# A graph network kernel: attention messages made by ScalarE as eight scaled copies per unit, and a one-hot build that reads its numbers from PSUM

## The reference, cut to what matters

```python
xl = x @ W
alpha = leaky_relu(a_src[src2] + a_dst[dst2] + a_edge)
ex = exp(alpha - segment_max(alpha, dst2)[dst2])
p = ex / segment_sum(ex, dst2)[dst2]
out = segment_sum(xl[src2] * p[..., None], dst2) + bias
```

## Time and profile before

| | us |
|---|---|
| median of 3 runs | 9410.33 |
| profiled execution | 9404.12 |
| its span | 9402.4 |
| POOL busy | 6718.0 (71%) |
| PE busy | 5202.7 (55%) |
| DVE busy | 3779.7 (40%) |
| ACT busy | 1844.8 (20%) |

### The profile page before, as it was taken

How to read it: one execution, slowest core, us unless ns; L and a number is a source line. 1 busy time by engine, 2 the same in 40 slices (tenths; PEclk the granted TensorE clock), 3 DMA queues, 4 the chain that set the end, 5 groups by cost and what they waited for, 6 DMA issues and landing times. The chain is left out here.

```text
span 9402.4 us, 110210 instructions
## 1 busy us (share of the span) xinstructions
PE 5202.7 (55%) x29965; PEld 3957.9 (42%) x29966; DVE 3779.7 (40%) x5860; ACT 1844.8 (20%) x2616; POOL 6718.0 (71%) x6802
## 2 busy tenths in 40 slices
PE   2777778777787778877512433424452243252443
PEld 1555555555565556655412322323331132242332
DVE  7444444444444444444412423324351243242436
ACT  1333333333333333333200000000010000000000
POOL 4777777777577777777377777777717777777772
PEclk6888887887777887777655666656665666666666
DMA  5222222222222222222322222222212222222221
GB/s 156 74 78 75 78 76 75 78 75 75 85 76 78 76 78 76 78 76 78 81 62 44 57 49 49 57 44 57 39 28 65 44 56 49 46 59 44 54 42 34
DMA packets 376814, 611.95 MB, mean 65 GB/s; under 512 B 173574, under 2 KB 211194, under 8 KB 374971
## 3 DMA queue, kind: packets, MB, share of 16 engines
q0 software_dynamic: 214032, 332.71, 16.9%
q1 hardware_dynamic: 144556, 255.75, 8.3%
q10 hardware_dynamic: 17945, 19.86, 0.7%
HBM read 575.04 MB, written 32.78 MB: 65 GB/s over the span
## 5 line engine op out<-in xcount | busy, mean ns | idle before, releaser
L1248 POOL DMA_INDIRECT big<-xl_table,idx_stage x3328 | 3335.8, 1002 | 1007.8 <-issue 997.7
L761 POOL DMA_INDIRECT big<-q_table,idx_stage x3328 | 3247.3, 976 | 1025.2 <-issue 953.7
L641 PE MATMUL bank<-zero_bf 1*128 1x512 bf16 (+1 forms) x1456 | 475.3, 399 | 2391.5 <-DVE wide L1369 2254.7
L868 PE MATMUL bank<-big,ident 128*128 128x512 f32 x1664 | 1204.1, 813 | 915.6 <-DMA big<-q_table,idx_stage 907.5
L872 PEld LDWEIGHTS bank<-big,wide 128*128 128x128 f32 x6656 | 1186.7, 251 | 561.6 <-issue 561.6
L872 PE MATMUL bank<-big,wide 128*128 x6656 | 1177.2, 336 | 0.0
L641 PEld LDWEIGHTS bank<-zero_bf 1*128 1x128 bf16 x1456 | 93.1, 97 | 2488.1 <-DVE wide L1369 2271.6
L1520 PEld LDWEIGHTS bank<-msg,onehot 128*128 128x128 f32 x6656 | 969.9, 232 | 260.4 <-issue 260.4
L1520 PE MATMUL bank<-msg,onehot 128*128 128x128 f32 (+1 forms) x6656 | 1033.7, 320 | 35.7 <-DVE onehot L626 35.3
L1303 DVE TENSOR_TENSOR work<-big,onehot_t 128x128 f32<-128x128 f32 x26 | 9.9, 379 | 2571.7 <-DMA big<-xl_table,idx_stage 2571.7
L886 PE MATMUL bank<-msg,onehot 128*128 128x67 f32 (+1 forms) x6656 | 1037.0, 308 | 11.4 <-DVE msg L815 11.4
(11 more groups left out here) (236 smaller groups left out, 4033.2 us busy)
## 6 DMA issues: line engine op xcount, KB each, us to landing
wide<-rel_rows SPq DMA_DIRECT2D x208, 512.0 KB, 3.7
big<-rel_rows SPq DMA_DIRECT2D x208, 512.0 KB
big<-q_table,idx_stage POOLq DMA_INDIRECT x3328
big<-xl_table,idx_stage POOLq DMA_INDIRECT x3328
edge_rows<-big SPq DMA_DIRECT2D x25, 257.0 KB, 6.0
xl_table<-big SPq DMA_DIRECT2D x12, 520.0 KB, 6.6
big<-in_edge_attr ACTq DMA_DIRECT2D x6, 1024.0 KB
wide<-in_edge_attr ACTq DMA_DIRECT2D x6, 1024.0 KB, 10.0
```

What stands on the lines that cost most here:

```text
L641: nc.tensor.matmul(banks[:, bank, :].rearrange("p (i c) -> p i c", c=pitch)[:, :, 0:width], k.zero_bf[:, :], k.zero_bf[:, 0:width].unsquee ...
L761: pool.indirect_dma_start(out=ring[:, group % UNROLL, s % GROUP, :], out_offset=None, in_=k.q_table, in_offset=bass.IndirectOffsetOnAxis(a ...
L868: nc.tensor.matmul(k.psum[u][:, :], k.ident[:, :], ring[:, u].rearrange("p i c -> p (i c)"), start=True, stop=False)
L1248: pool.indirect_dma_start(out=buf[p][:, s, :], out_offset=None, in_=k.xl_table, in_offset=bass.IndirectOffsetOnAxis(ap=k.idx_stage[:, s:s ...
```

## The change

In `gat_edges` DVE no longer makes messages. ACT makes them: after the copy of the weights it issues, for each of the unit's eight steps, one activation Copy of 64 columns with the edge's weight as scale, a column of one number per partition. The last of them signals `e_m`. The one-hot build takes its first operand from `numbers`, a copy of `iota` in PSUM bank 5, made once when the stage starts. What lay in bank 5 (the maxima's rows, the carries, the factor pair) moves to bank 4. For that, PE waits for DVE's factor (`s_fe`) before it writes the transposed weights over them. The wait on the sum of unit c - 2, which the message held on DVE, stands now before the one-hot build.

```diff
--- before.py
+++ after.py
@@ -1180,6 +1180,7 @@
     near = k.pairs[0][:, :, :].rearrange("p u c -> p (u c)")
     bank_ad = near.rearrange("p (s j) -> p s j", j=SLOT)
     near_sb = k.onehot_t[:, 1, 0:2, :].rearrange("p i c -> p (i c)").rearrange("p (s j) -> p s j", j=2)
+    numbers = k.psum[5][:, 0:P]
     LINKS = 28
     spread_bf = k.spread_bf[:, :, :].rearrange("p b j -> p (b j)")
     BIT = BUNITS // GAT_UNROLL
@@ -1261,7 +1262,8 @@
             nc.vector.memset(k.acc, 0.0).then_inc(e_acc, 1)
             nc.vector.memset(t_row[:, P:P + 1], BIG_NEG).then_inc(s_zero, 1)
             nc.vector.memset(u_row[:, P:P + 1], BIG_NEG).then_inc(s_zero, 1)
-            v.wait_ge(s_zero, 2)
+            nc.vector.tensor_copy(numbers, k.iota[:, :]).then_inc(s_zero, 1)
+            v.wait_ge(s_zero, 3)
 
             def turn_onehot(c, slot, pair, n):
                 v.wait_ge(s_rel[slot], pair * 16 + 16)
@@ -1317,7 +1319,7 @@
 
             def carries(b, link):
                 v.wait_ge(s_cr, b + 1)
-                link(nc.vector.tensor_copy(crow, k.psum[5][0:1, :]))
+                link(nc.vector.tensor_copy(crow, k.psum[4][0:1, :]))
                 nc.vector.tensor_tensor_scan(t_row[:, 1:P + 1], crow[:, 0:P], crow[:, P:2 * P], t_row[:, 0:1], ALU.add, ALU.max).then_inc(s_tu, 1)
                 nc.vector.tensor_tensor_scan(u_row[:, 0:P][:, ::-1], crow[:, 3 * P:4 * P][:, ::-1], crow[:, 2 * P:3 * P][:, ::-1],
                                              BIG_NEG, ALU.add, ALU.max).then_inc(s_tu, 1)
@@ -1326,8 +1328,8 @@
                 key = k.keys[:, ds(b * (P + 2), P + 2)]
                 rel = k.dst_rel[:, ds(b * P, P)]
                 v.wait_ge(s_tub, b + 1)
-                link(nc.vector.tensor_tensor(carry[:, 0:1], k.psum[5][:, 0:1], pen[:, 0:1], ALU.add))
-                link(nc.vector.tensor_tensor(carry[:, 1:2], k.psum[5][:, 1:2], pen[:, P:P + 1], ALU.add))
+                link(nc.vector.tensor_tensor(carry[:, 0:1], k.psum[4][:, 0:1], pen[:, 0:1], ALU.add))
+                link(nc.vector.tensor_tensor(carry[:, 1:2], k.psum[4][:, 1:2], pen[:, P:P + 1], ALU.add))
                 for side, edge in ((0, 1), (1, P)):
                     link(nc.vector.tensor_scalar(far, key[:, 1:P + 1], key[:, edge:edge + 1], BIG_NEG, ALU.not_equal, ALU.mult))
                     link(nc.vector.scalar_tensor_tensor(seg, far, carry[:, side:side + 1], seg, ALU.add, ALU.max))
@@ -1342,7 +1344,7 @@
                 v.wait_ge(s_exp, b + 1)
                 nc.vector.tensor_tensor(wx[:, 1, :], wx[:, 1, :], neq[:, 1:P + 1], ALU.mult).then_inc(s_w, 1)
                 v.wait_ge(s_fv, b + 1)
-                nc.vector.tensor_scalar(fac, k.iota_col[:, :], k.psum[5][:, 9:10], k.psum[5][:, 8:9], ALU.is_equal, ALU.mult).then_inc(s_fe, 1)
+                nc.vector.tensor_scalar(fac, k.iota_col[:, :], k.psum[4][:, 9:10], k.psum[4][:, 8:9], ALU.is_equal, ALU.mult).then_inc(s_fe, 1)
 
             def rescale(b):
                 start, = load_offsets(k, v, ACC_ROW, b * P + 1, 1, (NB - 1) * AW)
@@ -1353,7 +1355,6 @@
 
             def batch(b, p, turn):
                 first_unit = b * BUNITS
-                gather = buf[p]
                 link = Chain(v, s_ch, (b + 1) * LINKS)
 
                 def sums(it, first, last):
@@ -1368,18 +1369,13 @@
                         to = acc[:, ds(start, UNIT * AW)].rearrange("p (i c) -> p i c", c=AW)[:, :, 0:C + 2]
                         nc.vector.tensor_tensor(to, to, sums_of[c % SETS].rearrange("p (i c) -> p i c", c=P)[:, :, 0:C + 2], ALU.add).then_inc(e_acc, 1)
 
-                    def message(c):
-                        s = it * ITER + c * UNIT
+                    def spread(c):
                         wait(v, e_agg, n[c - 1])
-                        nc.vector.tensor_tensor(msg[c % SETS][:, :, 0:C], gather[:, s:s + UNIT, 0:C],
-                                                wsw[p][:, s:s + UNIT, 0:1].broadcast_to([P, UNIT, C]), ALU.mult).then_inc(e_m, 1)
-
-                    def spread(c):
-                        build_onehot(nc, k, onehot[c % SETS], step + c * UNIT).then_inc(e_S, 1)
+                        build_onehot(nc, k, onehot[c % SETS], step + c * UNIT, numbers).then_inc(e_S, 1)
 
                     for u in range(GAT_UNROLL):
                         if not begins(b):
-                            stages(u, first, last, (2, add), (0, message), (0, spread))
+                            stages(u, first, last, (2, add), (0, spread))
                         if spreads(b):
                             stages(u, first, last, (0, lambda c: turn_onehot(c, it % 2, (b + 2) * (BIT // 2) + it // 2, ahead)))
 
@@ -1438,6 +1434,9 @@
                         s = it * ITER + c * UNIT
                         wait(act, e_agg, n[c - 1])
                         nc.scalar.activation(msg[c % SETS][:, :, C:C + 2], wsw[p][:, s:s + UNIT, :], ACT.Copy).then_inc(e_w, 1)
+                        for i in range(UNIT):
+                            last_one = nc.scalar.activation(msg[c % SETS][:, i, 0:C], buf[p][:, s + i, 0:C], ACT.Copy, scale=wsw[p][:, s + i, 0:1])
+                        last_one.then_inc(e_m, 1)
 
                     for u in range(GAT_UNROLL):
                         if not begins(b):
@@ -1482,20 +1481,21 @@
             def ends_t(b):
                 pe.wait_ge(s_cc, 2 * b + 2)
                 for j in range(4):
-                    last = nc.tensor.transpose(k.psum[5][0:1, j * P:(j + 1) * P], cols[:, j:j + 1], k.ident[:, :])
+                    last = nc.tensor.transpose(k.psum[4][0:1, j * P:(j + 1) * P], cols[:, j:j + 1], k.ident[:, :])
                 last.then_inc(s_cr, 1)
 
             def carries_t(b):
                 pe.wait_ge(s_tu, 2 * b + 2)
-                nc.tensor.matmul(k.psum[5][:, 0:1], t_row[:, 0:P], k.ones_row[:, 0:1], start=True, stop=True)
-                nc.tensor.matmul(k.psum[5][:, 1:2], u_row[:, 1:P + 1], k.ones_row[:, 0:1], start=True, stop=True).then_inc(s_tub, 1)
+                nc.tensor.matmul(k.psum[4][:, 0:1], t_row[:, 0:P], k.ones_row[:, 0:1], start=True, stop=True)
+                nc.tensor.matmul(k.psum[4][:, 1:2], u_row[:, 1:P + 1], k.ones_row[:, 0:1], start=True, stop=True).then_inc(s_tub, 1)
 
             def factor_all(b):
                 pe.wait_ge(s_fb, 2 * b + 2)
-                nc.tensor.matmul(k.psum[5][:, 8:10], k.ones_row[:, :], fpair, start=True, stop=True).then_inc(s_fv, 1)
+                nc.tensor.matmul(k.psum[4][:, 8:10], k.ones_row[:, :], fpair, start=True, stop=True).then_inc(s_fv, 1)
 
             def weights_t(b):
                 pe.wait_ge(s_w, b + 1)
+                pe.wait_ge(s_fe, 2 * b + 1)
                 for j in range(2):
                     last = nc.tensor.transpose(k.psum[4][:, j * P:(j + 1) * P], wx[:, j, :], k.ident[:, :])
                 last.then_inc(s_wt, 1)
```

## The result

On one chip the changed kernel took 9233.09 us (median of 4 runs, 9221.46 to 9241.91) and the kernel before 9409.04 (4 runs, 9393.75 to 9411.84): a ratio of 0.9816 with its interval 0.9803 to 0.9828. The forecast was 9250. The profiled execution took 9229.47 us with a span of 9227.7, so 174.7 us less than the one of before. The build is still L626.

A forecast was written before the change was run, and what follows sets the result against it. POOL's gathers, issued without pause, plus a 70 us tail set each attention stage. 9404.1 − 194 (excess) + 34 (what stays) + 0 (tails) = 9244, median 6.2 above: 9250; range 9218 to 9285, or 9220 to 9325 with the first rival.

The forecast's parts named there:

- The bound and the excess: Attention stages: 1664 gathers by their period plus a 70 us tail; gather time over 944 ns each sums to 194.2 us.
- point at 0.13 us: About 0.13 us from its start a gather needs something and is held until the running DVE instruction ends.
- second point: Near its end a gather asks again; a compare with one scalar column holds it, ending 0.12 us before the gather.
- the rival by which the lengthening had another cause: DVE products and builds never held POOL's gathers; something else at the same times did; time stays at 9410; chance 4%.
- The forecast's own test: Reckoning on the kernel before: builds 141 us, products 28, short work 13, L1269 0 to 21; 182 to 203, measured 194.2.
- L1269: Turned compare in attention, one SBUF input and a scalar column: still holds gathers for 21 us, bounds 0 to 86.
- short work: DVE work on scores and maxima in 26 batches: some 0.5 us a batch, 13 us stays (0 to 25).
- the first rival: Freed from the build ahead, compare L1269 holds POOL as dearly as L803: saving only 95, 9315 us; chance 15%.
- The step: ACT's eight message copies per unit: 0.24 us from copy to copy, a unit of 2.1 us (1.4 to 3.0).
- The rival with ACT as the bound: The 8 scaled copies make ACT the bound, slower: tails grow from 0.31 us a copy, saving gone from 0.91; chance 4%.
- The 1.2 us that DVE was to be ahead by: Start of the last batch: DVE sheds four products between last gather and factors, two or so on the path, 1.2 us less.
- the 0.25 us of the forecast: Some 0.25 us of a DVE instruction's recorded time does not hold a gather; the rest does.

The follow-up runs named there:

- the halves: Two kernels, each with one part of the change against the kernel before: messages alone on ACT 9360.4 us, build alone from PSUM 9285.63 us.
- the doubled copies: Changed kernel with eight more scaled copies of 32 columns per unit on ACT, into an unused tile: 9279.04 us, ratio 0.9858.

## Why the prediction was right, step by step

**The bound and the excess.** Right. The attention stages lost 177.1 us, and 170.6 of them are gathers nearer to 944 ns. The forecast said 160 (194 down to 34).

**The build and the product hold by their two SBUF operands.** Shown: no lengthened gather ends 0.81 us after a build from PSUM, though 357 in the changed kernel and 208 in the kernel with the build alone have their point at 0.13 us under one; and the product with one operand in PSUM lengthens three of 218, by 0.08 us. A gather under a build from PSUM is still not always free. In the changed kernel 47 of the 357 take over 956 ns, 3.7 us together, most of them because the compare behind the build catches their second point (39 end 0.12 us after a compare, 3.4 us).

With this falls the rival by which the lengthening had another cause: the halves and the product from PSUM refute it. The Trainium skill's inference that descriptor generation isn't stalled by a tensor_tensor ("SBUF — State Buffer", Who interferes with whom) does not stand here: in the kernel before, builds hold 168 gathers for 124.0 us and products 189 for 49.4. The Trainium skill's other sentence in that section, that a DVE instruction with two SBUF inputs contends with a GpSimd instruction that reads SBUF, is what the runs show.

**The prices of the halves.** The forecast's own test gave 141 for the builds and 28 for the products. In the kernel before they hold 124.0 and 49.4, so the test came near the measured 194.2 by two errors that cancel; that agreement was luck. Builds standing alone hold 142.2 us. Products standing alone hold 52.0, nearly twice the term: with a product of 0.69 us and gathers at random phases some 131 of 376 should be caught (0.435 / 1.25), and 189 were, for 275 ns each in place of 218 (half of 0.435). A likely reason, not tested, is that the phases are tied: POOL is let go when a DVE instruction ends and asks again 0.81 + 0.30 + 0.13 = 1.24 us later. So that term was mis-sized, and it did no harm: both halves were removed, and only what was left entered the sum.

**What stays.** Forecast 34 us: L1269 21 and short work 13. Measured 23.5. The compare (L1271) holds 97 gathers at the first point for 10.9 us and 48 at the second, which end 0.12 us after it, for 4.2: 15 us in place of 21. The other 8, where 13 were counted, are short work and a few ns over 944 each. Both terms were too high, by 10 us together, the compare's within its bounds of 0 to 86. The compare did not take the place of the build as the first rival had it: it holds 145 gathers for 0.10 us each, where L803 in the second convolution stage makes 43.0 us.

**A term that was missing.** POOL's index copies shrank too: 26 of L1240 took 13.7 us before and take 7.1 now, mean 527 and 274 ns. DVE held them as it held the gathers: the eight long ones before, 1127 to 1209 ns, all end 0.09 us after a build, and the mean is 528 ns with the messages alone on ACT and 275 with the build alone from PSUM. All index copies together gave 6.5 us, which the forecast had at nothing. 10 from what stays and 6.5 from the copies are the 17 us between 160 and 177.

**ACT.** Right at the chosen value. The step was guessed at 0.24 from bounds of 0.15 to 0.35; eight copies take 2.00 us with the last at 333 ns, so a step of (2.00 − 0.333)/7 = 0.238. A unit is 2.2 with the weights. An estimate from the Trainium skill's figures ("ScalarE: Activation LUTs", What ACT_TABLE_LOAD costs) is 332 ns for one and a step of 0.24; the trace agrees on both. The 204 ns of L847, which the forecast called an agreement, lie 18 ns above the fixed part that it quotes. The rival with ACT as the bound is as far off as was said; the doubled copies show where it begins, in the tails.

**The tails.** Unit length 2.51 us, as forecast. Three closes of a span in the first stage's tail:

```profile
6821.99 0.20 PE L648 MATMUL bank<-zero_bf 1*128 1x1 bf16 x2
...
6824.50 0.20 PE L648 MATMUL bank<-zero_bf 1*128 1x1 bf16 x2
...
6827.02 0.20 PE L648 MATMUL bank<-zero_bf 1*128 1x1 bf16 x2
```

The start of the last batch was half right:

```profile
6804.28 0.28 DVE L1347 TENSOR_SCALAR work<-iota_col,bank 128x1 f32<-128x1 f32 x1 [0.38 <-PE bank L1494]
...
6804.71 0.66 PE L1500 MATMUL bank<-ident,work 128*128 128x128 f32 x2 [0.47 <-DVE work L1347]
...
6805.96 2.00 ACT L1438 ACTIVATE msg<-big,work 128x64 f32<-128x64 f32 x8
...
6808.09 1.22 PE L1520 MATMUL bank<-msg,onehot 128*128 128x128 f32 x4 [1.71 <-ACT msg L1436]
```

PE's transposes now wait for the factor, as the diff says. From the last gather's end to the first segment sum it is 6808.09 − 6781.4 = 26.7 us, against 6890.03 − 6864.1 = 25.9: 0.8 later where 0.6 was forecast. The 1.2 us that DVE was to be ahead by did not appear: the factor starts 22.9 us after the last gather in both. All in all the two stretches behind the last gathers are even 0.5 and 1.4 us shorter, near the 0 of the forecast.

**The total.** 9404.1 − 160 + 6 gave 9250. What came was 177 in the attention stages, 10 given back by the convolution stages, 6 gained ahead of them, and 2 in the tails. That is 15 us more than forecast, for a profiled execution of 9229.5; the median of the runs is 9233. The 10 and 6 are of the size by which the same code differs between runs, and that they nearly cancel is luck: the first convolution stage has 2151.7 to 2157.0 us over five kernels of the second and third chip that leave it alone.

## What to carry to other kernels

If an engine issues indirect DMAs back to back and sets a stage's length, look at the longest of its DMAs and at what ends a fixed time before they do. A DVE tensor_tensor of two SBUF operands there costs POOL time as well as DVE, and reading one operand from PSUM or moving the work to ACT takes that away. Cutting such instructions in pieces worked for builds and compares (another 97 us beyond the changed kernel, to 0.9718 of the kernel before) and failed where product pieces came ahead of build pieces, so each such chain has to be measured. Read the effect from the stage that the engine bounds, since a chip with another bottleneck shows none of it in the total.

## What the runs showed of the hardware that was not expected

- The kernel before takes 9409.04 us where the result was taken, 9406.64 and 9417.09 on the second and third chip, and 10872.19 on the first. A unit of the tail can take 2.51 us there too, but for long stretches PE starts one instruction in 0.70 us, its segment sums take 362 ns in the mean in place of 320, and the mean granted clock is 0.647 in place of 0.71.
- A whole DVE instruction holds a gather only if the gather's point at 0.13 us lies some 0.2 us or more after the instruction's recorded start: with the messages alone on ACT, builds lengthen 2 of 37 gathers with the point within 0.15 us and 309 of 315 from 0.20 us on. That is the 0.25 us of the forecast, a little shorter. It fits that pieces help in the convolution stages: a gather is let go before the next piece begins to hold. It does not explain the chains.
- A chain of pieces can hold a gather through all of them: the 2.72 us above is one of 75.
- POOL's own small copies are held like the gathers: 246 ns alone, up to 1209 in the kernel before.
